# Relative attention stage: another place for four transposes a head, for the relative scores, the row sums and half of the window exponentials, and another order on POOL and on the sync queue

## The chip, the cores and the metric

The kernel runs on one core of a Trainium2 chip. The metric is device time in microseconds (us) for one execution of the whole program; the median of the runs is what is compared. The engines are called PE (TensorE, with its weight loads as PEld), DVE (VectorE), ACT (ScalarE), POOL (GpSimd) and SP (the engine that only issues DMAs here).

## What is computed

A transformer layer: attention with relative positions, then a plain attention and a mixture of experts. The change is in the first part alone. Cut to it (the input x is 2 x 2048 x 256, so there are 2 x 16 = 32 heads of 2048 rows, each 16 wide):

```
B, S, H, NH, MRP = (4, 256, 256, 16, 64)
DK = H // NH
def _rel_idx(seq_len):
    r = jnp.arange(seq_len)
    dist = r[None, :] - r[:, None]
    return jnp.clip(dist, -MRP, MRP) + MRP
nb, seq_len, _ = x.shape
idx = _rel_idx(seq_len)
rk = embK[idx]
rv = embV[idx]
...
logits = jnp.einsum('bhqd,bhkd->bhqk', q, k) + jnp.einsum('bhqd,qkd->bhqk', q, rk)
w = jax.nn.softmax(logits, axis=-1)
out = jnp.einsum('bhqk,bhkd->bhqd', w, v) + jnp.einsum('bhqk,qkd->bhqd', w, rv)
out = out.transpose(0, 2, 1, 3).reshape(nb, seq_len, NH * DK)
return out @ Wo.T + bo
```

Further than 64 columns from the diagonal the relative terms are constants of their side, so they are folded into two versions of k and v. Only a window of 128 columns left and 128 right of each 128-row tile needs the table itself.

## The kernel before

The stage is `rel_attention`. It makes one pass over the 32 heads in a loop of four unrolled heads (p = 0 to 3, eight turns of the loop). One pass through the body for head t is called a period here. In it the engines work on three heads at once: the exponentials and the weighted sum of head t, the maxima of head t+1, and the relative scores of head t+2.

PE sets the beat. A period has 16 steps; each step holds one `weigh` (p times v, L1422), two units of scores for the maxima (L1351, two halves each, into the two buffers psA), and four or five items of RING, which fill the three banks of psS. RING has 68 items a head: 56 blocks of transposed scores for the exponentials ("E", L1391), 8 transposes of the window exponentials ("W", L1397) and 4 transposes of the folded window ("F", c = 0 to 3, L1402). The fills run LEAD = 8 items ahead, so item i stands near step (i - 8) / 4.25. An F fill waits in PE's order for POOL's fold of the same c. Between the units stand four products R (L1361) with the relative table, in the steps of R_STEPS, behind their `weigh`.

DVE takes every psA buffer in PE's order as a turn, 38 a period: 32 maxima (L1225, L1227), the four R copies (`keep_r`, L1244), the gathering of the heads (L1258) and the row of maxima (L1251). After the turns of SUM_TURNS it sums the right half of the window (`sum_right`, L1238), and after turn RC_REL of every second head it inverts the denominators. ACT empties psS (`copy_out`, L1318, an exponential or a copy) and takes the 16 window exponentials of a head between those (`window_exp`, L1322), eight of them ahead, in steps 12 to 15 of the period before, and eight in the period itself.

Two paths lead through DRAM, since they skew rows. For c = 0 to 3:

- scores of head t+2: R copied by DVE, `write_r` (L1010), `read_r` (L1016) once the write has landed and DVE is done with group c of the head before, then `part_r` on POOL (L1137), which masks left and right.
- window of head t: `join_p` on POOL (L1137, L1172) when ACT's exponentials of group c are there, `write_p` (L1020), `read_p` (L1025) when that has landed, `fold_p` on POOL (L1180, L1184), then the F fill on PE.

All these DMAs are issued by SP, in one written order, and so are `load_stack` (nine DMAs of q and k for a head, twice a period), `load_v` (once in four heads), `send_m` (the row of maxima, L1031), and for every second head `gather_denominators` (L1039, L1042), `spread_reciprocals` (L1047, L1050) and `store_o` (L1060). A `wait` in one of them holds whatever is behind it in SP's order. Likewise POOL's order of joins, parts and folds is written out.

## Time and profile before

| | us |
|---|---|
| median of 3 runs | 5036.89 (5022.62 to 5041.27) |
| the profiled execution | 5042.24, its span 5040.5 |
| PE busy, whole span | 4249.3 (84%) |
| DVE busy | 3690.0 (73%) |
| ACT busy | 3016.6 (60%) |
| POOL busy | 1447.1 (29%) |

The relative attention takes the stretch from about 0.25 ms to 2.53 ms; the plain attention and the experts after it are not touched. Shares over the whole span say little, since the stages have different limits. What counts is a single period in the steady part, read engine by engine, with the waits that end last there. Times below are often given as a phase: us since the start of the first `weigh` (step 0) of that period. The head shown most starts at 1236.55 us and is an odd one (p = 1, without the denominators); the next one, even (p = 2), starts at 1301.56 us.

### The profile page before, as it was taken

What the parts mean: (1) busy time and instruction counts of PE and PEld (TensorE: products, weight loads), DVE (VectorE), ACT (ScalarE), POOL (GpSimd) and SP (SyncE); (2) the same over time, 40 slices, a digit from 0 to 9 for tenths busy, and PEclk for the clock granted to TensorE, in tenths of its full rate; (3) what the DMA queues carried; (4) which work ended last, traced back from release to release, by engine and by line L of the source; (5) the groups of instructions that cost most, each with busy time, mean ns of one, the idle gap of its engine ahead of it and who ended that gap; (6) DMA issues with size and microseconds to landing.
All of it is one profiled execution on the core that took longest, in us unless ns stands there. A gap on an engine that the chain in (4) does not pass through costs nothing. (4 is left out here: it accounts for less than half of the span.)

```text
span 5040.5 us, 97058 instructions
## 1 busy us (share of the span) xinstructions
PE 4249.3 (84%) x26882; PEld 2231.3 (44%) x26882; DVE 3690.0 (73%) x6635; ACT 3016.6 (60%) x5838; POOL 1447.1 (29%) x1418
## 2 busy tenths in 40 slices
PE   3778888888888888888846699999999999669997
PEld 1334444444444444444433233333333333459997
DVE  2776777677767676767726788888888888557775
ACT  1226666666666666666601187787787778336664
POOL 0034545554545545545410000000000000142232
PEclk9958889898988888988977699999999999779999
DMA  3755556565656555565554532333223322476664
GB/s 103 229 113 131 129 134 147 132 143 128 139 121 143 137 136 133 135 135 130 132 161 163 113 48 37 44 43 48 39 36 48 49 39 38 103 222 172 171 178 120
DMA packets 512589, 579.74 MB, mean 115 GB/s; under 512 B 71976, under 2 KB 451928, under 8 KB 502000
## 3 DMA queue, kind: packets, MB, share of 16 engines
q1 hardware_dynamic: 453568, 489.90, 43.0%
q10 hardware_dynamic: 38656, 58.73, 3.1%
q0 software_dynamic: 19824, 24.52, 3.0%
q8 instruction: 264, 4.33, 0.4%
q14 instruction: 277, 2.27, 0.2%
HBM read 365.10 MB, written 210.95 MB: 114 GB/s over the span
## 5 line engine op out<-in xcount | busy, mean ns | idle before, releaser
L1225 DVE TENSOR_REDUCE ra_pm<-ra_psA 128x1 f32<-128x896 f32 x1068 | 1162.2, 1088 | 478.5 <-PE ra_psA L1351 462.4
L1318 ACT ACTIVATE ra_p<-ra_psS 128x512 f32<-128x512 f32 x2053 | 1116.2, 604 | 535.0 <-PE ra_psS L1391 275.6
L633 DVE TENSOR_REDUCE pa_pm<-pa_psA 128x2 f32<-128x1024 f32 x1068 | 1261.0, 1219 | 183.6 <-PE pa_psA L724 183.2
L698 ACT ACTIVATE pa_p<-pa_psS 128x512 f32<-128x512 f32 x2054 | 1072.1, 602 | 290.7 <-PE pa_psS L747 263.6
L1351 PE MATMUL ra_psA<-ra_zs,ra_qs 48*128 48x512 f32 x2136 | 918.7, 496 | 111.3 <-DVE ra_rst L1244 58.0
L724 PE MATMUL pa_psA<-pa_zs,pa_qs 48*128 48x512 f32 x2136 | 837.4, 476 | 76.1 <-DVE pa_recb L664 29.9
L747 PE MATMUL pa_psS<-pa_qs,pa_zs 50*128 50x512 f32 x2056 | 823.8, 469 | 51.7 <-ACT pa_p L698 35.2
L1391 PE MATMUL ra_psS<-ra_qs,ra_zs 50*128 50x512 f32 (+3 forms) x2184 | 769.9, 433 | 54.8 <-ACT ra_p L1318 47.6
L1422 PE MATMUL ra_psO<-ra_p,ra_vs 128*32 128x512 f32 (+3 forms) x6400 | 622.1, 497 | 0.0
L747 PEld LDWEIGHTS pa_psS<-pa_qs,pa_zs 50*128 50x128 f32 x2056 | 348.2, 188 | 595.6 <-ACT pa_p L698 562.4
L758 PE MATMUL pa_psO<-pa_p,pa_vs 128*32 128x512 f32 x4096 | 557.6, 617 | 0.0
L1391 PEld LDWEIGHTS ra_psS<-ra_qs,ra_zs 50*128 50x128 f32 x2184 | 363.7, 195 | 363.8 <-ACT ra_p L1318 296.6
L1351 PEld LDWEIGHTS ra_psA<-ra_zs,ra_qs 48*128 48x128 f32 x2136 | 378.6, 202 | 320.2 <-DVE ra_pm L1227 122.8
L724 PEld LDWEIGHTS pa_psA<-pa_zs,pa_qs 48*128 48x128 f32 x2136 | 366.7, 192 | 247.8 <-DVE pa_pm L633 148.7
L612 POOL COPY pa_vs<-pa_vall 128x256 f32 (+1 forms) x33 | 13.2, 399 | 1310.6 <-PE pa_psO L758 1074.6
L2224 PE MATMUL mo_psH<-mo_hp,mo_w_parts 128*128 128x384 f32 x1392 | 284.5, 340 | 5.9 <-DVE mo_w_parts L2310 5.9
L2238 PE MATMUL mo_psY<-mo_w_parts,mo_hid_parts 128*128 128x256 f32 x2088 | 283.7, 281 | 0.0
L2238 PEld LDWEIGHTS mo_psY<-mo_w_parts,mo_hid_parts 128*128 128x128 f32 x2088 | 272.3, 189 | 3.8 <-DVE mo_hid_parts L2380 0.2
L1180 POOL TENSOR_TENSOR ra_blk<-ra_blk 128x508 f32<-128x508 f32 x128 | 161.8, 1264 | 381.1 <-DMA ra_blk<-window_rows 376.1
L1422 PEld LDWEIGHTS ra_psO<-ra_p,ra_vs 128*32 128x32 f32 x6400 | 203.9, 114 | 147.8 <-ACT ra_p L1318 54.6
L2195 POOL DMA_INDIRECT acc_rows<-mo_y,mo_ids x87 | 154.2, 1772 | 384.4 <-DVE mo_y L2365 366.7
L1137 POOL TENSOR_TENSOR ra_pc<-ra_sw,masks 128x512 f32<-128x512 f32 (+2 forms) x160 | 169.4, 1059 | 277.8 <-DVE ra_sr L1238 248.5
(250 smaller groups left out, 5306.6 us busy)
## 6 DMA issues: line engine op xcount, KB each, us to landing
relative_rows<-ra_rst SPq DMA_DIRECT2D x136, 512.0 KB, 4.0
ra_blk<-window_rows SPq DMA_DIRECT2D x128, 512.0 KB, 4.6
mo_w_raw<-ffn_W SPq DMA_DIRECT2D x58, 1024.0 KB, 5.5
ra_dl<-relative_rows SPq DMA_DIRECT2D x136, 256.0 KB, 3.2
window_rows<-ra_pc SPq DMA_DIRECT2D x128, 256.0 KB, 4.3
pa_qs<-q_halves SPq DMA_DIRECT2D x210, 128.0 KB, 5.5
pa_zs<-kl_halves SPq DMA_DIRECT2D x210, 128.0 KB, 5.9
ra_qs<-q_halves SPq DMA_DIRECT2D x204, 128.0 KB, 3.8
```

What stands on the lines that cost most here:

```text
L633: dve.reduce_max(pm[:, par, 2 * a:2 * a + 2], psA[w][:, :, :], AX.X).then_inc(s_am.h, 1)
L698: act.activation(pr[:, i % NPR, :], psS[:, slot(i), :], ACT.Exp).then_inc(s_ex.h, 1)
L724: last = pe.matmul(psA[w][:, half, :], qs[0:PR, k % U, i * P:(i + 1) * P], zs[0:PR, k % U, e * G:(e + 1) * G], start=True, stop=True)
L747: pe.matmul(psS[:, slot(i), :], zs[at:at + PR + NP2, p % U, z * P:(z + 1) * P], qs[at:at + PR + NP2, p % U, c * G:(c + 1) * G], start=True ...
L758: last = pe.matmul(psO[32 * m:32 * m + 32, :], vs[:, p % 2, 4 * (k % 4) + m, :], pr[:, (4 * k + m) % NPR, :], start=k % 4 == 0, stop=k % 4 ...
L1225: dve.reduce_max(pm[:, q, i, 2 * left:2 * left + 1], psA[w][:, lo:lo + 2 * G - P], AX.X).then_inc(s_far.h, 1)
L1318: act.activation(dst, psS[:, slot(i), :], ACT.Exp if kind == "E" else ACT.Copy).then_inc(s_cp.h, 1)
L1351: last = pe.matmul(psA[w][:, half * G:(half + 1) * G], qs[0:PR, q, i * P:(i + 1) * P], zs[0:PR, q, at:at + G], start=True, stop=True)
L1391: last = pe.matmul(dst[:, lo:hi], zs[at:at + PR + NP2, q, z * P:(z + 1) * P], qs[at:at + PR + NP2, q, c * G + lo:c * G + hi], start=True, ...
L1422: last = pe.matmul(psO[32 * m:32 * m + 32, lo:hi], v[:, z, :], pr[:, (4 * k + m) % NPR, lo:hi], start=n == 0, stop=n == 3, tile_position=( ...
L2224: last = pe.matmul(psH[:, u % 3, 0:BT], w1[:, q, x, c, f * P:(f + 1) * P], hp[:, q, z, c, :], start=c == 0 and m == 0, stop=c == CH - 1 an ...
L2238: last = pe.matmul(psY[:, j, 0:D], hid[:, x, u % NHID, j * P:(j + 1) * P], w2[:, q, z, f, :], start=f == 0 and m == 0, stop=f == FC - 1 an ...
```

## The change

No instruction is added or removed. Six things are moved:

- The four F fills go from ring places 32, 41, 50, 59 to 38, 43, 52, 63.
- R goes from steps 0, 1, 4, 5 to steps 0, 3, 6, 8.
- The second eight window exponentials go from two a step in steps 0 to 3 to one a step in steps 0 to 7; the eight ahead stay.
- The four sums go from turns 8, 10, 12, 14 to 5, 9, 14, 25, the inversion from turn 20 to 17.
- SP's order is another one, and so is POOL's.

```
-for _c, _at in reversed(tuple(enumerate((32, 40, 48, 56)))):
+for _c, _at in reversed(tuple(enumerate((38, 42, 50, 60)))):
     RING.insert(_at, ("F", _c, 0))
-R_STEPS = (0, 1, 4, 5)
+R_STEPS = (0, 3, 6, 8)
-WX_STEP, WX_PER = 12, 2
+WX_STEPS = (12, 12, 13, 13, 14, 14, 15, 15) + tuple(range(STEPS, STEPS + 8))
-RC_REL = 20
-SUM_TURNS = (8, 10, 12, 14)
+RC_REL = 17
+SUM_TURNS = (5, 9, 14, 25)
...
-        k, ahead = WX_STEP + j // WX_PER, 1
+        k, ahead = WX_STEPS[j], 1
...
                     read_r(t + 2, p, 0)
-                    write_r(t + 2, p, 1)
+                    if p % 2 == 0:
+                        gather_denominators(t, n)
                     write_p(t, p, 1)
                     read_p(t, p, 0)
-                    write_p(t, p, 2)
+                    write_r(t + 2, p, 1)
                     read_p(t, p, 1)
                     read_r(t + 2, p, 1)
-                    write_p(t, p, 3)
+                    write_p(t, p, 2)
                     if p % 2 == 0:
-                        gather_denominators(t, n)
+                        spread_reciprocals(n)
                     write_r(t + 2, p, 2)
-                    write_r(t + 2, p, 3)
                     if p == 2:
                         load_v(t + 2, 4 * (t + 2))
+                    read_p(t, p, 2)
                     read_r(t + 2, p, 2)
-                    read_p(t, p, 2)
-                    if p % 2 == 0:
-                        spread_reciprocals(n)
-                    read_p(t, p, 3)
+                    write_r(t + 2, p, 3)
+                    write_p(t, p, 3)
                     read_r(t + 2, p, 3)
                     load_stack(t + 3, p + 1, 0, s_qa)
+                    read_p(t, p, 3)
                     send_m(t + 1, p + 1)
...
-                    for c in range(4):
-                        join_p(t, p, c)
-                    for c in range(2):
-                        part_r(t + 2, c)
-                    for c in range(4):
-                        fold_p(t, c)
-                    for c in range(2, 4):
-                        part_r(t + 2, c)
+                    join_p(t, p, 0)
+                    join_p(t, p, 1)
+                    part_r(t + 2, 0)
+                    join_p(t, p, 2)
+                    fold_p(t, 0)
+                    fold_p(t, 1)
+                    part_r(t + 2, 1)
+                    part_r(t + 2, 2)
+                    join_p(t, p, 3)
+                    fold_p(t, 2)
+                    fold_p(t, 3)
+                    part_r(t + 2, 3)
```

What that makes of SP's queue in the later part of an even head (p = 0). The semaphores s_rw2 and s_pw3 tell that `write_r` 2 and `write_p` 3 have landed, s_rec that the denominators are inverted. Before:

```order
L1010 DMA relative_rows<-ra_rst 128x4x256 [waits ra_s_rc]
...
L1016 DMA ra_dl<-relative_rows 128x4x128 [waits ra_s_am,ra_s_rw2]
...
L1025 DMA ra_blk<-window_rows 128x4x256 [waits ra_s_fl,ra_s_pw2]
...
L1047 DMA reciprocals<-ra_rec 128x32 [waits ra_s_rec]
...
L1025 DMA ra_blk<-window_rows 128x4x256 [waits ra_s_fl,ra_s_pw3]
...
L1016 DMA ra_dl<-relative_rows 128x4x128 [waits ra_s_am,ra_s_rw3]
...
L995 DMA ra_zs<-kl_halves 16x1984 x3
...
L1031 DMA ra_qs<-ra_mrow 1x16x128 [waits ra_s_mr]
```

and in the changed kernel:

```order
L1047 DMA reciprocals<-ra_rec 128x32 [waits ra_s_rec]
...
L1010 DMA relative_rows<-ra_rst 128x4x256 [waits ra_s_rc]
...
L1025 DMA ra_blk<-window_rows 128x4x256 [waits ra_s_fl,ra_s_pw2]
...
L1016 DMA ra_dl<-relative_rows 128x4x128 [waits ra_s_am,ra_s_rw2]
...
L1020 DMA window_rows<-ra_pc 128x4x128 [waits ra_s_pc]
...
L1016 DMA ra_dl<-relative_rows 128x4x128 [waits ra_s_am,ra_s_rw3]
...
L995 DMA ra_zs<-kl_halves 16x1984 x3
...
L1025 DMA ra_blk<-window_rows 128x4x256 [waits ra_s_fl,ra_s_pw3]
...
L1031 DMA ra_qs<-ra_mrow 1x16x128 [waits ra_s_mr]
```

The reciprocals now stand ahead of `write_r` 2, and the last `read_p` now stands behind the nine DMAs of `load_stack`.

POOL, the last join of a head (the one with 128x384 in it) and what stands ahead of it. Before:

```order
L1172 TENSOR_TENSOR ra_pc<-ra_pc,ra_tmp 128x512 [waits ra_s_ps]
...
L1137 TENSOR_TENSOR ra_pc<-ra_sw,masks 128x512 [waits ra_s_sr,ra_s_pw1,ra_s_we]
...
L1137 TENSOR_TENSOR ra_tmp<-ra_sw,masks 128x384 [waits ra_s_ps]
...
L1137 TENSOR_TENSOR ra_dr<-ra_dl,masks 128x512 [waits ra_s_rr0]
```

and in the changed kernel:

```order
L1137 TENSOR_TENSOR ra_dr<-ra_dl,masks 128x512
L1137 TENSOR_TENSOR ra_dl<-ra_dl,masks 128x512
...
L1137 TENSOR_TENSOR ra_pc<-ra_sw,masks 128x512
...
L1137 TENSOR_TENSOR ra_tmp<-ra_sw,masks 128x384
...
L1172 TENSOR_TENSOR ra_pc<-ra_pc,ra_tmp 128x512
...
L1180 TENSOR_TENSOR ra_blk<-ra_blk 128x4x127
L1184 TENSOR_TENSOR ra_blk<-ra_blk,ra_sr 128x4
```

The last join now stands behind `part_r` 2 (the first two rows), and the folds 2 and 3 stand right behind that join.

## Rows read from the trace of the kernel before

**Rows 1.** Busy time in stretches (us, busy, instructions; PEclk is the granted clock).

```profile
core 0: us, PE busy (x) PEld busy (x) DVE busy (x) ACT busy (x) POOL busy (x), PEclk, DMA share, GB/s
1236.50:1301.50 65.00, 57.66 (x415) 28.65 (x413) 49.00 (x108) 44.39 (x90) 33.91 (x37) 0.89 0.59 135
1256.20:1269.80 13.60, 10.15 (x40) 4.45 (x38) 6.47 (x13) 3.21 (x6) 10.34 (x12) 0.50 0.64 190
```

**Rows 2.** Who waited for whom, whole span (us in total, times, longest).

```profile
POOL ra_pc L1137 <- DVE ra_sr L1238: 248.5, 32, 15.6
...
PE ra_psS L1402 <- POOL ra_blk L1184: 136.5, 32, 6.3
```

**Rows 3.** The tile ra_nm, written once a head.

```profile
L1234 DVE TENSOR_REDUCE ra_nm<-ra_pm x33: 219/220/222, 316.1 to 2493.1; 128x16 f32<-128x64 f32 x33
```

**Rows 4.** Timeline of PE, head at 1236.55: start, length, operation, idle before.

```profile
1236.55 1.07 PE L1422 MATMUL ra_psO<-ra_p,ra_vs 128*32 128x512 f32 x8
...
1252.16 1.07 PE L1422 MATMUL ra_psO<-ra_p,ra_vs 128*32 128x512 f32 x8
...
1257.31 1.94 PE L1422 MATMUL ra_psO<-ra_p,ra_vs 128*32 128x512 f32 x8
...
1266.03 1.09 PE L1402 MATMUL ra_psS<-ident,ra_blk 128*128 128x128 f32 x4 [3.44 <-POOL ra_blk L1184]
...
1291.21 1.06 PE L1422 MATMUL ra_psO<-ra_p,ra_vs 128*32 128x512 f32 x8
...
1301.56 1.07 PE L1422 MATMUL ra_psO<-ra_p,ra_vs 128*32 128x512 f32 x8
```

**Rows 5.** Timeline of POOL, the same head: last join, parts 0 and 1, first fold.

```profile
1254.29 1.28 POOL L1137 TENSOR_TENSOR ra_pc<-ra_sw,masks 128x512 f32<-128x512 f32 x1 [0.24 <-POOL ra_pc L1172]
...
1258.72 1.27 POOL L1137 TENSOR_TENSOR ra_dr<-ra_dl,masks 128x512 f32<-128x512 f32 x1 [0.18 <-POOL ra_pc L1172]
...
1261.67 1.27 POOL L1137 TENSOR_TENSOR ra_dr<-ra_dl,masks 128x512 f32<-128x512 f32 x1
...
1264.35 1.25 POOL L1180 TENSOR_TENSOR ra_blk<-ra_blk 128x508 f32<-128x508 f32 x1
```

**Rows 6.** Timeline of SP, the same head: first write and read, last read, stack, maxima.

```profile
1239.57 0.40 SPq L1010 DMA_DIRECT2D relative_rows<-ra_rst  x1
...
1245.89 0.36 SPq L1016 DMA_DIRECT2D ra_dl<-relative_rows  x1
...
1281.20 0.36 SPq L1016 DMA_DIRECT2D ra_dl<-relative_rows  x1
1281.99 1.33 SPq L995 DMA_DIRECT2D ra_qs<-q_halves  x3
...
1286.55 1.20 SPq L1031 DMA_DIRECT2D ra_qs<-ra_mrow  x2
```

**Rows 7.** Timeline of SP, the even head at 1301.56: v loads and reciprocals.

```profile
1329.29 0.79 SPq L1003 DMA_DIRECT2D ra_vg<-v_rows  x1
...
1334.15 0.45 SPq L1016 DMA_DIRECT2D ra_dl<-relative_rows  x1
...
1339.89 0.34 SPq L1047 DMA_DIRECT2D reciprocals<-ra_rec  x1
...
1344.42 0.39 SPq L1025 DMA_DIRECT2D ra_blk<-window_rows  x1
```

**Rows 8.** DMA issues: operation, count, KB each, median us to landing.

```profile
relative_rows<-ra_rst SPq DMA_DIRECT2D x136, 512.0 KB, 4.0
ra_blk<-window_rows SPq DMA_DIRECT2D x128, 512.0 KB, 4.6
...
ra_dl<-relative_rows SPq DMA_DIRECT2D x136, 256.0 KB, 3.2
...
ra_qs<-ra_mrow SPq DMA_DIRECT2D x66, 8.0 KB, 5.9
pa_qs<-pa_mrow SPq DMA_DIRECT2D x66, 8.0 KB, 1.8
```

**Rows 9.** Timeline of DVE, the same odd head: a copy of R between turns.

```profile
1254.04 1.22 DVE L1244 COPY ra_rst<-ra_psA 128x1024 f32<-128x1024 f32 x1
```

**Rows 10.** Timeline of PE at the edge of the loop body (fourth head to first).

```profile
1162.59 0.50 PE L1351 MATMUL ra_psA<-ra_zs,ra_qs 48*128 48x512 f32 x1 [2.95 <-issue]
```

## The prediction

> **What bounds the kernel now.** The change touches one stage, so I left the shares of the whole span aside and read in this order: how long a head takes, which engine is full within a head, where that engine waits, and which chain ends last at that wait. The row of maxima is made once a head, 33 times from 316.1 to 2493.1 us [rows 3]: 32 periods of 68.0 us, 2177 us in all. An undisturbed odd head goes from the weigh at 1236.55 to that at 1301.56, 65.0 us [rows 4]. In it PE is busy for 57.66 us, DVE 49.00, ACT 44.39, POOL 33.91 [rows 1]. So PE is the bound, and nobody else is near 65. What PE loses lies in one place. At phase 29.5 (1266.03) the transpose F of c = 0 comes after 3.44 us of idle time, released by POOL's fold [rows 4]; over all heads that wait is 136.5 us in 32 times, 4.3 us a head [rows 2]. Around it the granted clock is 0.50, that is 1.2 instead of 2.4 GHz, from 1256.2 to 1269.8, with 10.15 us of PE work in it [rows 1]. Once in four heads the loop's edge costs 2.95 us more and a slow stretch [rows 10].
>
> The chain behind the wait: POOL makes the fold at 1264.35, behind four joins and two parts [rows 5], and the joins themselves were late, since join 2 waits for DVE's sum 0 (248.5 us in 32 times, 7.8 us a head [rows 2]). This idle time of POOL ends in the wait of PE.
>
> **What PE would take without waits.** Step 4 begins at phase 15.6 (1252.16). The last three steps, from 1291.21 to 1301.56, run at full clock with two transposes W in them and take 10.35 us [rows 4], 3.45 us a step. Fifteen point six and twelve such steps are 57 us. That is 8 us a head, 256 us in all, to be had if nothing else is late.
>
> **Part by part.** *The edits with one answer.* The eight exponentials move from steps 0 to 3 to steps 0 to 7. ACT has 20 us of idle time in a head [rows 1] and the work is the same; W of c = 2 stands in step 9 and wants its four by step 3. I cost it at nothing; if ACT's cover is gone, it is one exponential, half a microsecond, and no more. The sums 0 and 1 come earlier and cost DVE the same; join 2 can then start some 5 us earlier, and fold 0 stands behind three joins and one part instead of four and two. F0 itself moves 6 ring items later. So the wait of 4.3 us goes; I take that as certain, for fold 0 is then ready near phase 21 (odd heads) or 22 (even), and F0 is wanted near 25.
>
> *R two to three steps later.* The third R was DVE's turn 12, at 1254.04, phase 17.5, ahead of any slow stretch [rows 9]: 1.46 us a turn. It is turn 16 now, so it starts near 23.3 and is copied by 24.6. The least would be 16 turns of 1.22 us, the length of that copy, ready by 20.7; the most is that a slow stretch stays, 28. I take 24.6, by the nearest row.
>
> *What now stands in a row behind it.* `write_r` 2 at 24.8, landed 4.0 later; `read_r` 2, landed 3.2 later [rows 8]; `part_r` 2 on POOL, 2.7 us like part 1 (1261.67 to 1264.35); then join 3, which the change has put behind that part, 4.4 us (1254.29 to 1258.72) [rows 5]. Join 3 is done at J = 39.1. Fold 2 needs 1.5 us more, so F2 is free at 40.7, while it is wanted in step 10, behind its weigh, near 37.5. A wait of some 3 us.
>
> In even heads the reciprocals stand ahead of `write_r` 2. The inversion is behind turn 17, so done near 26.2. The spreading holds SP from 1339.89 to 1344.42, 4.5 us [rows 7], until 30.7. Then J = 30.9 + 4.0 + 3.2 + 2.7 + 4.4 = 45.2. In one head of four `load_v` stands there too, 1329.29 to 1334.15, 4.9 us [rows 7]; `read_r` 2 is then issued at 36.7 instead of 34.9, and J = 47.0. In before the same wait for the reciprocals held only the last `read_p`, and nobody waited for that.
>
> *The last read behind the stack.* This weighs most. With join 3 done at J, SP issues `write_p` 3, `read_r` 3, then nine DMAs of the stack (1281.99 to 1286.4), then `read_p` 3: from `read_r` 3 to there is 5.3 us (1281.20 to 1286.55) [rows 6], so J + 5.8. How long it takes to land the trace does not show in this place. Alone it takes 4.6 us. The row of maxima, 8 KB, issued behind the same stack, takes 5.9, and 1.8 in the other attention, where no such stack is ahead of it: 4.1 us of queueing [rows 8], and 4.6 + 4.1 = 8.7. The first `write_r`, 512 KB behind the other stack, was waited for from 1239.57 to 1245.89, 6.3 us [rows 6], though issued a microsecond further behind. I take 7.5, between the two, with 4.6 and 9.5 as ends. Then fold 3, 1.5 us: F3 is free at J + 14.8. PE wants it in step 13, two and a half steps after F2, at J + 1.6 + 8. A second wait of 5 us. Who is queued behind it on PE: everything of three more steps.
>
> *From F3 to the end of the head.* As in before from 1291.21 to 1301.56, 10.35 us, and 1.0 for F3 and the rest of its step: 11.4. The wait brings a slow clock. In before it stayed at 0.50 from the restart at 1266.03 to 1269.8 [rows 1, 4], 3.8 us that count half: 1.9. I take 2.0.
>
> **The sum.** A head takes J + 14.8 + 11.4 + 2.0 = J + 28.2: 67.3 for each of two odd heads, 73.4 and 75.2 for the even ones, against 65.0 in before, the loop's edge being left as it is. That is 2.3 + 2.3 + 8.4 + 10.2 = 23.2 us in four heads, eight times: 186 us. On the profiled execution's 5042 us this gives 5228, and against the median, 5 us lower, 5223.
>
> So the gain of 4.3 us at F0 is real, and is given back at F2 and F3.
>
> **Rivals.** (1) *The clock stays low for longer.* If two waits in a head hold it at 0.50 for as much work as in before, 10.15 us of it, 5.1 us are lost instead of 2.0: 3.1 x 32 = 99 us more, 5322. For it: in before the clock fell ahead of the wait, in a stretch full of R and W. Against: R is now spread over steps 0 to 8. The Trainium skill's page "TensorE: Matmul & The Clock Gate", section Terms, prices a throttled stretch at its length times (1 - K/N), half here. On the 13.6 us stretch that would be 6.8 us, and the time 5223 + 4.8 x 32 = 5377; the trace has PE idle for 3.4 us of that stretch, so I stay with 5.1.
>
> (2) *The reads are quick enough.* If `read_p` 3 lands in 4.6 us, as alone (2.9 less), and there is no slow stretch (2.0 less), 0.9 of the mean 5.8 us a head is left; R a microsecond sooner takes it away. The time is then 5037, no change. For it: the DMA queues are only 0.59 busy [rows 1]. Against: the 5.9 us of the 8 KB row.
>
> (3) *PE runs free: faster.* Were fold 3 done by phase 46 and fold 2 by 37.5, a head would take 57 us and the kernel 5037 - 256 = 4781. It decides at `read_p` 3: it must be issued by phase 38 or so, when in SP's order even join 3 is not done. Half of that gain, 4910, would need the chain from R to join 3 shorter by 6 us. Turns at 1.22 us would give 4.
>
> (4) *The F0 wait stays.* It would only add; fold 0 has 3 us to spare, so I give it nothing of its own.
>
> **How the numbers follow.** The forecast has 58 in 100, the longer slow stretch 18, no change 10, faster 14 (all the way 6, part of it 8). 0.5% (25 us) is about what a measurement of this kernel tells from no change. So slower by over that: 0.76; within it: 0.10; faster: 0.14. Ends of the unknown terms: the landing -2.9 or +2 us a head (-93, +64), the slow stretch -2 or +3.1 (-64, +99), R up to -4. The range goes from 5020 to 5340; it leaves out the faster cases and the far end of the first rival.
>
> **What would show it.** In the profile after: the wait of PE's F fill on POOL's fold should be no less than in before, 250 us or so in 60 times, and stand at c = 2 and 3; POOL should wait for the last `read_p` for about 10 us a head; POOL's wait for DVE's sum should be gone; SP's last `read_p` should stand behind the stack with 7 us or more to landing; heads should be 67 and 73 to 75 us long in turn. The prediction is wrong if F3 finds its fold done, or if even heads are no longer than odd ones.

## The result: slower by 6.6%, 1.8 times the loss forecast

| | before | after |
|---|---|---|
| median, us | 5037.3 (5022.62 to 5041.27, 4 runs) | 5369.16 (5340.55 to 5382.8, 4 runs) |
| ratio to before | | 1.0657, 95% interval 1.0609 to 1.0705 |
| relative attention, first to last row of maxima, us | 2177.0 | 2457.2 |
| the same for each of 32 heads | 68.0 | 76.8 |

The forecast was 5223 (5020 to 5340): slower, as it came out, but by 186 us where 332 were lost. All rows below are of the profiled executions, 5042.24 us before and 5340.55 after: the second is the quickest of its four, so there are 298 us between them, and not 332. The page of the profile after, its first lines and the granted clock in 40 slices:

```profile
span 5338.8 us, 97058 instructions
...
PE 4370.9 (82%) x26882; PEld 2307.9 (43%) x26882; DVE 3692.3 (69%) x6635; ACT 3046.6 (57%) x5838; POOL 1446.8 (27%) x1418
...
PEclk9868888787878887887867769999999999869999
```

PE's share of the span fell, and yet PE is busy 122 us longer, with no instruction added. The stage alone, by after's row of maxima (before's is [rows 3]):

```profile
L1238 DVE TENSOR_REDUCE ra_nm<-ra_pm x33: 219/220/222, 318.3 to 2775.5; 128x16 f32<-128x64 f32 x33
```

The window between its ends, with the columns of [rows 1], in before:

```profile
316.10:2493.10 2177.00, 1891.82 (x13120) 937.37 (x13120) 1576.40 (x3477) 1415.16 (x2797) 1130.37 (x1175) 0.87 0.59 136
```

and in after:

```profile
318.30:2775.50 2457.20, 2000.58 (x13124) 1010.73 (x13128) 1576.99 (x3475) 1444.64 (x2798) 1129.66 (x1173) 0.81 0.54 120
```

The stage is 280 us longer. PE is busy for 109 us of that, and the granted clock went from 0.87 to 0.81. The rest is waiting. Who waited for whom (us in total, times, longest), after, whole span:

```profile
POOL ra_blk L1180 <- DMA ra_blk<-window_rows: 524.2, 65, 17.3
...
PE ra_psS L1406 <- POOL ra_blk L1184: 260.9, 56, 9.5
```

In after's stage alone, PE for POOL (the folds) and for DVE (the copies of R, the maxima):

```profile
PE ra_psS L1406 <- POOL ra_blk L1184: 253.9, 55, 9.5
PE ra_psA L1355 <- DVE ra_rst L1248: 82.4, 130, 3.2
PE ra_psA L1355 <- DVE ra_pm L1231: 55.7, 83, 1.7
```

and the last two in before, in its stage (its waits for the folds all lie in the stage):

```profile
PE ra_psA L1351 <- DVE ra_rst L1244: 43.2, 66, 3.2
...
PE ra_psA L1351 <- DVE ra_pm L1227: 20.5, 69, 0.5
```

PE's wait for the folds was 136.5 us in 32 times [rows 2] and is 260.9 in 56, 253.9 of it in the stage: 117 more there. Of after's waits, 108 us stand in step 10 (fold 2) and 153 in step 12 (fold 3). PE's waits for DVE, which copies R and takes the maxima, went from 64 to 138 us: 74 more. 109 + 117 + 74 = 300, against 280; PE's waits for ACT got 12 us shorter (47 to 35), and I did not follow the last 8. POOL's wait for DVE's sum [rows 2] is gone; it waits for the reads of the window instead, 524 us (376 in before).

Windows of after, an odd head from 1341.2 (the first five) and the late part of the even one from 1413.9:

```profile
1341.20:1363.20 22.00, 19.90 (x159) 10.15 (x157) 18.34 (x39) 16.15 (x32) 15.73 (x15) 1.00 0.88 193
1363.20:1369.60 6.40, 4.99 (x31) 2.49 (x29) 5.06 (x11) 4.09 (x8) 4.18 (x5) 0.82 0.29 97
1369.60:1380.00 10.40, 9.94 (x56) 5.16 (x55) 5.36 (x11) 4.44 (x8) 4.60 (x4) 0.50 0.25 77
1380.00:1395.00 15.00, 14.07 (x97) 7.19 (x97) 11.32 (x29) 10.38 (x22) 3.40 (x5) 0.85 0.69 139
1395.00:1401.40 6.40, 0.07 (x2) 0.04 (x1) 1.12 (x3) 0.80 (x2) 1.47 (x3) 0.74 0.56 109
...
1453.50:1462.70 9.20, 0.09 (x5) 0.05 (x1) 1.64 (x4) 0.04 (x1) 7.94 (x8) 0.64 0.23 74
1462.70:1476.90 14.20, 11.68 (x59) 6.00 (x60) 6.96 (x17) 8.04 (x16) 1.52 (x3) 0.50 0.82 139
1476.90:1492.20 15.30, 14.56 (x81) 6.96 (x81) 7.70 (x18) 9.65 (x20) 6.86 (x8) 0.68 0.24 43
```

The odd head has two faults. In the second row a step of 6.4 us holds only 5 us of PE's work, and the clock falls in it (at 1367.3), ahead of any wait for a fold; the third row is at 0.50 (1.2 GHz) with PE busy for 9.94 of 10.4 us. And in the fifth row PE does nothing for 6.3 us. The even head waits for 9 us from 1453.5, and then runs at 0.50 and 0.68 until it ends. PE's timeline at these places (columns of [rows 4]):

```profile
1365.98 0.49 PE L1355 MATMUL ra_psA<-ra_zs,ra_qs 48*128 48x512 f32 x1 [1.00 <-DVE ra_pm L1231]
...
1401.37 1.12 PE L1406 MATMUL ra_psS<-ident,ra_blk 128*128 128x128 f32 x4 [6.33 <-POOL ra_blk L1184]
...
1462.68 1.09 PE L1406 MATMUL ra_psS<-ident,ra_blk 128*128 128x128 f32 x4 [9.12 <-POOL ra_blk L1184]
```

What lies behind F3 in the odd head, on POOL:

```profile
1380.82 1.27 POOL L1172 TENSOR_TENSOR ra_pc<-ra_pc,ra_tmp 128x512 f32<-128x512 f32 x1
...
1399.78 1.25 POOL L1180 TENSOR_TENSOR ra_blk<-ra_blk 128x508 f32<-128x508 f32 x1 [16.06 <-DMA ra_blk<-window_rows]
```

and on SP:

```profile
1379.78 0.36 SPq L1010 DMA_DIRECT2D relative_rows<-ra_rst  x1
1382.12 0.38 SPq L1020 DMA_DIRECT2D window_rows<-ra_pc  x1
1386.31 0.36 SPq L1016 DMA_DIRECT2D ra_dl<-relative_rows  x1
1387.42 1.34 SPq L995 DMA_DIRECT2D ra_qs<-q_halves  x3
...
1391.85 0.41 SPq L1025 DMA_DIRECT2D ra_blk<-window_rows  x1
```

and on DVE, the last of the 32 maxima of head t+1:

```profile
1384.92 1.09 DVE L1229 TENSOR_REDUCE ra_pm<-ra_psA 128x1 f32<-128x896 f32 x1 [2.44 <-PE ra_psA L1355]
1385.93 0.28 DVE L1231 CUSTOM_DVE_ANT_0 ra_sw<-ra_psA,ra_dl 128x128 f32<-128x128 f32 x1
```

The last join is done at J = 1382.09. `write_r` 3 has landed by 1382.67, but `read_r` 3 also waits for DVE to be done with the group that it overwrites: the last maximum is done at 1386.2, the read goes out at 1386.31. The stack stands behind it, and `read_p` 3 is issued at 1391.85, J + 9.8 (the median of such heads is J + 7), and has landed by 1399.78. So the chain is the one forecast, with more in it.

**A measure of the clock for what follows.** Each trace has a record of granted clock. I counted in the stage how long it stood at 0.50: 575 us in before, 18.0 a head, and 950 us in after, 29.7 a head. (The windows give about the same: 2 x (1 - 0.87) x 68.0 = 17.7 and 2 x (1 - 0.81) x 76.8 = 29.2.) PE was busy for 448 and 783 us of that; half of it, 7.0 and 12.2 us a head, is my estimate of what the clock cost, since a `weigh` of eight matmuls takes 1.07 us at 1.00 and 1.93 at 0.50.

### The profile page after: what moved, and what is told of

The parts are those of the page before. It is cut to its first block and busy times, and to the rows that moved or that the text cites. A ratio compares the mean times of both kernels' runs of the same rounds, so it can differ in the third digit from the quotient of the medians.

```text
span 5338.8 us, 97058 instructions
## 1 busy us (share of the span) xinstructions
PE 4370.9 (82%) x26882; PEld 2307.9 (43%) x26882; DVE 3692.3 (69%) x6635; ACT 3046.6 (57%) x5838; POOL 1446.8 (27%) x1418
## 5 line engine op out<-in xcount | busy, mean ns | idle before, releaser
L1355 PE MATMUL ra_psA<-ra_zs,ra_qs 48*128 48x512 f32 x2136 | 948.4, 524 | 182.4 <-DVE ra_rst L1248 98.4
L1395 PE MATMUL ra_psS<-ra_qs,ra_zs 50*128 50x512 f32 (+3 forms) x2184 | 833.6, 469 | 38.7 <-ACT ra_p L1322 35.5
L1426 PE MATMUL ra_psO<-ra_p,ra_vs 128*32 128x512 f32 (+3 forms) x6400 | 676.1, 536 | 0.0
L1355 PEld LDWEIGHTS ra_psA<-ra_zs,ra_qs 48*128 48x128 f32 x2136 | 414.1, 220 | 395.5 <-DVE ra_rst L1248 158.8
L1395 PEld LDWEIGHTS ra_psS<-ra_qs,ra_zs 50*128 50x128 f32 x2184 | 408.8, 217 | 338.7 <-ACT ra_p L1322 185.7
L1406 PE MATMUL ra_psS<-ident,ra_blk 128*128 128x128 f32 x512 | 118.3, 373 | 261.3 <-POOL ra_blk L1184 260.9
L1137 POOL TENSOR_TENSOR ra_dr<-ra_dl,masks 128x512 f32<-128x512 f32 (+2 forms) x170 | 179.4, 1055 | 517.2 <-DMA ra_dl<-relative_rows 510.3
L1426 PEld LDWEIGHTS ra_psO<-ra_p,ra_vs 128*32 128x32 f32 x6400 | 221.2, 121 | 157.7 <-ACT ra_p L1322 64.9
```

Source lines behind the costliest of these rows:

```text
L1355: last = pe.matmul(psA[w][:, half * G:(half + 1) * G], qs[0:PR, q, i * P:(i + 1) * P], zs[0:PR, q, at:at + G], start=True, stop=True)
L1395: last = pe.matmul(dst[:, lo:hi], zs[at:at + PR + NP2, q, z * P:(z + 1) * P], qs[at:at + PR + NP2, q, c * G + lo:c * G + hi], start=True, ...
L1426: last = pe.matmul(psO[32 * m:32 * m + 32, lo:hi], v[:, z, :], pr[:, (4 * k + m) % NPR, lo:hi], start=n == 0, stop=n == 3, tile_position=( ...
```

## The experiments

"Slow" is the time at 0.50 a head, "F waits" PE's wait for the folds over the whole span. Each ratio is to the kernel before, run beside it (its medians there were 5033 to 5048). The interval of c1 is wide because its four runs go from 4893.86 to 4975.79.

| run | median us | ratio (95%) | stage | slow | F waits |
|---|---|---|---|---|---|
| before | 5037.3 | | 2177.0 | 18.0 | 136.5 |
| after | 5369.16 | 1.0657 | 2457.2 | 29.7 | 260.9 |
| a1 | 5146.14 | 1.0212 (1.0170 to 1.0255) | 2282.4 | 22.7 | 130.4 |
| a2 | 5276.28 | 1.0457 (1.0416 to 1.0499) | 2421.1 | 31.6 | 190.8 |
| a3 | 5246.63 | 1.0402 (1.0360 to 1.0444) | 2372.3 | 28.3 | 171.6 |
| a4 | 5004.85 | 0.9944 (0.9917 to 0.9970) | 2126.5 | 17.8 | 9.2 |
| a5 | 4932.82 | 0.9804 (0.9777 to 0.9831) | 2041.1 | 11.4 | 22.7 |
| a6 | 5074.74 | 1.0078 (1.0051 to 1.0105) | 2209.1 | 23.5 | 8.3 |
| b1 | 5055.96 | 1.0027 (0.9991 to 1.0062) | 2175.8 | 22.6 | 38.6 |
| b2 | 4887.29 | 0.9695 (0.9667 to 0.9723) | 2013.6 | 11.1 | 21.1 |
| c1 | 4906.64 | 0.9769 (0.9691 to 0.9848) | 2018.0 | 12.3 | 3.0 |
| c2 | 4898.31 | 0.9705 (0.9663 to 0.9747) | 2035.0 | 11.5 | 32.0 |
| c3 | 5294.96 | 1.0514 (1.0459 to 1.0569) | 2417.5 | 28.0 | 237.8 |
| c4 | 5359.88 | 1.0568 (1.0487 to 1.0649) | 2461.3 | 27.6 | 72.3 |
| d1 | 5354.04 | 1.0603 (1.0569 to 1.0637) | 2471.1 | 32.6 | 261.1 |
| d2 | 4885.03 | 0.9689 (0.9663 to 0.9715) | 2024.4 | 11.9 | 25.0 |
| d3 | 5391.61 | 1.0692 (1.0647 to 1.0738) | 2506.0 | 34.9 | 244.8 |

### From after backwards: the three places in the queues

**a1**, the last read ahead of the stack on SP:

```
                     read_r(t + 2, p, 3)
-                    load_stack(t + 3, p + 1, 0, s_qa)
                     read_p(t, p, 3)
+                    load_stack(t + 3, p + 1, 0, s_qa)
```

> The changed kernel with one edit: the last read of the window rows is issued ahead of the nine DMAs of the stack, as before the change, and nothing else. In the changed kernel that read was issued 7.2 us after the last join and took 8.2 to 9 us to land. Theory 1 (the second wait of PE in a head, at the fold of c = 3, is made by this read's place behind the stack): issued at some 4.2 us after the join, since it then waits for the landing of the write, and landed 5 us later, the fold is ready 6 us sooner; the wait of PE there nearly goes, with part of the slow clock: 5369 falls by 5 to 8 us a head, to 5110 to 5210. Theory 2 (the low clock of 24 to 31 us a head comes from the new spread of relative products and transposes over the steps, whatever is waited for): 5340 or more, the slow stretches as long as they are.

Measured: 223 us of the 332 are back. `read_p` 3 is issued at phase 43.3 to 43.5 in odd heads and 50.4 to 51.8 in even ones, and lands 4.7 us later; in after it was issued at 48 and at 52.8 to 54.2, and took 8.0 to 9.0. PE's wait for the folds is halved (waits, as above):

```profile
PE ra_psS L1406 <- POOL ra_blk L1184: 130.4, 32, 10.3
```

130 us of wait went, and 223 us of time; the slow stretches went from 29.7 to 22.7 us a head with it. What went is the wait in step 12, for fold 3: 153 us before, 4 now; that in step 10, for fold 2, is 127 us (108). The last read behind the stack is the largest single part of the loss.

**a2**, the reciprocals back behind `read_r` 2:

```
-                    if p % 2 == 0:
-                        spread_reciprocals(n)
                     write_r(t + 2, p, 2)
...
                     read_r(t + 2, p, 2)
+                    if p % 2 == 0:
+                        spread_reciprocals(n)
```

> The changed kernel with one edit: the spreading of the reciprocals goes behind the third read of the relative rows, and nothing else. Theory 1 (even heads are longer because it stands ahead of the third write of the relative rows and holds the sync queue until 31 us): the last join of an even head comes 6 us sooner, and the even heads are as long as the odd ones: 16 heads by 6 us, about 100 us, 5270. Theory 2 (even heads are longer by something else, the clock or the loads of v): over 5340, the last join of even heads where it was, at 46 to 48 us.

Measured: 93 us back. The last join of even heads is now done at 41.7 to 43.7 instead of 47 to 48. The slow time did not fall (31.6).

**a3**, the last join ahead of `part_r` 2 on POOL:

```
                     part_r(t + 2, 1)
-                    part_r(t + 2, 2)
                     join_p(t, p, 3)
+                    part_r(t + 2, 2)
```

> The changed kernel with one edit: on POOL the last join stands ahead of the third part of the relative rows, and nothing else. Theory 1 (the join is late because of that part, which waits for a read of what DVE copies in step 6): the last join is done near 30 us instead of 41 to 48, the wait of PE at c = 2 is gone (3.4 us in odd, 9 us in even heads), while the last read still stands behind the third and fourth relative reads and the stack, so it lands near 53 and PE still waits at c = 3: 5369 less some 6 us a head, 5180. Theory 2 (POOL's order matters little, since the join also waits for the exponentials that come one a step): the last join at 36 or later and 5330 or more.

Measured: 123 us back. The last join now starts its add at 29 to 34.6, but F3 still waits, for its read stands behind `read_r` 3 and the stack: an early join is worth only part of the loss while SP's order holds the read. (The three singles add up to 439 us, more than the 364 of the three together: they share some of the waiting.)

**a4**, all three:

> The changed kernel with the three edits of the other runs together: the last window read ahead of the stack, the reciprocals behind the third relative read, the last join ahead of the third part. Ring places, steps of the relative products, exponentials, sums and the rest of both orders are as changed. Theory 1 (the ring and the turns are sound, only the queues behind them are not): both waits of PE go, the slow clock shrinks to the loop's edge, and a head takes 57 to 60 us: 4780 to 4900, under the kernel before. Theory 2 (the clock falls because of the spread of relative products and transposes): the waits go but 15 us or more of slow clock a head stay, and the time is 5050 or more.

Measured: 364 us back and the kernel 0.6% faster than before; the wait for the folds in its trace:

```profile
PE ra_psS L1406 <- POOL ra_blk L1184: 9.2, 8, 2.5
```

and the window of its stage:

```profile
318.80:2445.30 2126.50, 1900.73 (x13117) 952.83 (x13119) 1572.08 (x3476) 1442.42 (x2797) 1131.30 (x1173) 0.87 0.60 139
```

So three places in two written orders make the whole loss. The time lies between the two that were written down for it, 4780 to 4900 and 5050 or more. Left in a4 are the later R, the F places, the sums and the exponentials, and a clock no better than before's, though PE hardly waits for a fold any more.

**a5**, a4 with the third sum three turns later, out of the turns of the third R:

```
-SUM_TURNS = (5, 9, 14, 25)
+SUM_TURNS = (5, 9, 17, 25)
```

> The combined version (last window read ahead of the stack, reciprocals behind the third relative read, last join ahead of the third part), with one more edit: DVE's sum 2 behind turn 17 instead of turn 14, out of the way of the relative product of step 6, which in every head has a wait of 1.0 us at phase 24.8 and makes step 6 last 5.4 us. Theory 1 (queues alone): the combined version less 0.6 us a head, 4985. Theory 2 (a crowded step makes the clock fall: 17 us of slow clock from phase 26 on in some heads): these stretches from phase 26 on go as well, 4900 to 4960.

Measured: 72 us more, 2.0% faster than before; PE's wait for the maxima in the stage fell by a third and the clock rose to 0.91, in the window of its stage:

```profile
316.60:2357.70 2041.10, 1820.21 (x13124) 925.91 (x13128) 1568.92 (x3475) 1437.20 (x2798) 1133.55 (x1173) 0.91 0.62 145
```

**a6**, a4 with the exponentials back at two a step:

```
-WX_STEPS = (12, 12, 13, 13, 14, 14, 15, 15) + tuple(range(STEPS, STEPS + 8))
+WX_STEPS = (12, 12, 13, 13, 14, 14, 15, 15) + (16, 16, 17, 17, 18, 18, 19, 19)
```

> The combined version with the second eight window exponentials back at two a step in steps 0 to 3. If the spreading of the exponentials is worth nothing by itself, as predicted: 5005 within 25. If it relieves ACT where ACT is full: steps 0 to 3 longer, 5030 or more. If it keeps the last join and ACT's steps 4 to 7 late: 4980 or less.

Measured: 70 us slower than a4. So in a4's setting the spread of the exponentials is worth 70 us; it was costed at nothing. The likely way, not tested by itself, is that two of them a step push back ACT's emptying of psS: step 0 of every fourth head (p = 3) took 5.3 us instead of 3.8, eight slow stretches begin in step 0 where a4 has none, and the slow time grew to 23.5 us a head.

### From before forwards: one part alone

**b1**, the kernel before with the F places of after:

```
-for _c, _at in reversed(tuple(enumerate((32, 40, 48, 56)))):
+for _c, _at in reversed(tuple(enumerate((38, 42, 50, 60)))):
```

> The kernel before with one edit: the four F transposes at the ring places of the changed kernel (38, 43, 52, 63 for 32, 41, 50, 59). F0 is wanted some 6 items, 5 us, later, and POOL's fold is where it was, at phase 29. Theory 1 (PE's wait at F0 is worth its own length and the slow clock behind it): the wait shrinks from 4.3 us a head to about 1 or none, the slow clock of 10 to 14 us with it, 5037 falls to 4850 to 4930. Theory 2 (the slow stretch starts at phase 19.5, ahead of the wait, and is made by the dense steps of R and W; the wait only fills it): 4980 to 5010, the slow clock stays at 10 us or more a head.

Measured: no change, 1.0027 (0.9991 to 1.0062), above both expectations. The wait is mostly gone:

```profile
PE ra_psS L1402 <- POOL ra_blk L1184: 38.6, 13, 3.0
```

and the stage is as long as it was:

```profile
316.60:2492.40 2175.80, 1981.87 (x13125) 999.23 (x13129) 1578.52 (x3477) 1424.82 (x2798) 1130.85 (x1174) 0.83 0.59 136
```

98 us of wait became 90 us more of PE's busy time, with the same instructions: the clock fell from 0.87 to 0.83. What is left of the wait is 13 waits of about 3 us, all in step 6. One of them, in PE's timeline:

```profile
1170.68 1.08 PE L1402 MATMUL ra_psS<-ident,ra_blk 128*128 128x128 f32 x4 [2.96 <-POOL ra_blk L1184]
```

and the windows ahead of it, of it and behind it:

```profile
1163.00:1167.00 4.00, 3.76 (x27) 1.77 (x25) 4.00 (x7) 2.34 (x5) 3.59 (x5) 1.00 0.42 124
1167.70:1170.70 3.00, 0.04 (x2) 0.05 (x1) 0.77 (x3) 0.81 (x2) 2.77 (x4) 0.94 0.56 184
1170.70:1184.00 13.30, 13.30 (x68) 6.67 (x68) 6.66 (x16) 5.98 (x11) 2.85 (x4) 0.50 0.53 159
```

The clock falls at the end of the wait and stays at 0.50 for 13.3 us in which PE is never idle. It does so at all 13: it falls within the last 0.9 us of the wait and comes back 9.3 to 13.5 us behind it (once 3.4).

**b2**, the kernel before with folds 0 and 1 ahead of parts 0 and 1 on POOL:

```
                         join_p(t, p, c)
                     for c in range(2):
+                        fold_p(t, c)
+                    for c in range(2):
                         part_r(t + 2, c)
-                    for c in range(4):
+                    for c in range(2, 4):
                         fold_p(t, c)
```

> The kernel before with one edit: on POOL the folds 0 and 1 stand ahead of the parts 0 and 1 (still behind the four joins). Fold 0 is then done near phase 24 instead of 29, F0 is wanted near 25. Theory 1: the same gain as by moving F0, 4850 to 4930. Theory 2 (dense steps make the slow stretch): 4980 to 5010. If the parts, now 3 us later, held DVE at the groups 0 and 1 of the head after next, it would be slower; they are wanted from step 10 on, phase 45, and done by 27, so neither theory expects it.

Measured: 3.0% faster than before, faster than every kernel here but d2, its twin. In the head from 1155.9, on POOL:

```profile
1177.99 1.27 POOL L1180 TENSOR_TENSOR ra_blk<-ra_blk 128x508 f32<-128x508 f32 x1
```

on PE:

```profile
1179.69 0.63 PE L1404 MATMUL ra_psS<-ident,ra_blk 128*128 128x128 f32 x4 [0.47 <-POOL ra_blk L1184]
```

and the window around it:

```profile
1177.90:1185.00 7.10, 6.61 (x61) 3.66 (x60) 6.31 (x13) 4.53 (x9) 6.37 (x9) 1.00 0.89 274
```

The fold starts at phase 22.1 instead of 27.8 [rows 5], F0 waits for 0.47 us instead of 3.44 [rows 4], and the clock stays at 1.00 throughout this head. 115 us of wait went, and 150 us of time. The crowded step is as it was: 19 of the 33 slow stretches of b2 begin in step 4, against 27 of 51 in before.

**c1**, b2 with the F places of after (the edit of b1):

> The kernel before with the folds 0 and 1 ahead of the parts 0 and 1 (4887 us by itself) and also the ring places of the changed kernel (no gain by themselves, 5056, though PE's wait fell from 136.5 to 38.6 us). Theory 1 (the ring places only matter through the wait at F0; that is gone already): 4887 within 25. Theory 2 (the transposes crowd the other steps at the new places and make the clock fall): 4930 or more, with a longer slow clock than the 12 us a head of the fold run.

**c2**, b2 with `R_STEPS = (0, 1, 3, 6)`:

> The kernel before with the folds 0 and 1 first, and the relative products in steps 0, 1, 3, 6 instead of 0, 1, 4, 5, so that none of them shares a step with a transpose of the window after step 1. Theory 2 (the clock falls after a crowded step: in the fold run it falls at phase 19.5, after step 4 with a product and a transpose): the slow stretches from phase 19 on go, 4800 to 4850. Theory 1 (only waits matter; there is none at phase 19): 4880 to 4900.

Measured: c1 0.9769 (0.9691 to 0.9848), c2 0.9705 (0.9663 to 0.9747), against 0.9695 of b2. Neither adds anything. But c1 and b1 have the same F places and differ in POOL's order alone, and c1 is 149 us faster. In its stage:

```profile
PE ra_psS L1404 <- POOL ra_blk L1184: 3.0, 2, 1.6
```

```profile
317.30:2335.30 2018.00, 1845.31 (x13124) 936.35 (x13128) 1578.34 (x3476) 1418.33 (x2798) 1133.26 (x1174) 0.90 0.64 147
```

The clock is 0.90 against b1's 0.83, PE is busy 137 us less, and no slow stretch begins in step 6, where b1 has 13. So the F places do not lower the clock by themselves: what b1 lost there came with the late fold and the 3 us waits that it left.

**c3**, b2 with `R_STEPS = (0, 3, 6, 8)`, those of the change:

> The kernel before with the folds 0 and 1 first, and the relative products at the changed kernel's steps 0, 3, 6, 8; the queues' order is of before. The fourth write of the relative rows waits until phase 33 and stands ahead of two reads of the window rows in the sync queue. Theory 1 (later products alone make the late chain, whatever the queue's order): fold 2 at 41 or later, wanted at 38: a wait of 3 us or more a head, 4950 to 5050. Theory 2 (the products spread over free steps make it shorter, the wait stays under 1 us): 4880 or less.

Measured: 408 us slower than b2, nearly as slow as after, with SP's order of before; both times written down for it (4950 to 5050, 4880) are missed. PE's waits, of which 108 us stand in step 5 (F0) and 130 in step 9 (F2):

```profile
PE ra_psS L1404 <- POOL ra_blk L1184: 237.8, 64, 7.6
```

A later R, then, does the same harm without the change's orders: the written queue of before holds `read_p` 0 behind `write_r` 1 and `read_p` 2 behind `write_r` 3. In heads p = 1, `write_r` 3 is now issued at 42.9 and `read_p` 2 at 44.0, against 26.6 in b2; POOL's wait for the reads of the window is 548 us, against 219. In a4 the same R steps stand beside an order with `read_p` 2 ahead of `write_r` 3, and it is issued at 27.2. The later R and the orders have to be judged together.

### What lowers the clock

**c4**, after, with eight useless matmuls ahead of F2 and sixteen ahead of F3, into the bank that F overwrites. They are added work, of no use to the result:

```
+                    for _ in range((0, 0, 8, 16)[c]):
+                        pe.matmul(dst, zs[64:64 + PR + NP2, q, 0:P], qs[64:64 + PR + NP2, q, 0:G], start=True, stop=True)
```

> The changed kernel with 8 more matmuls ahead of the transpose F2 and 16 ahead of F3 of every head, of 512 columns and 0.22 us each at full clock (1.8 and 3.5 us), into the bank that the transposes then overwrite, ahead of the wait for the fold: PE does useless work where it stood idle. Nothing else is changed, and the folds are ready when they are. Theory 1 (the idle time itself makes the slow clock of 26 us a head, of which the busy part is lost by half): the slow clock shrinks by 10 us or more a head and the time falls by 2 to 5 us a head, to 5200 to 5300. Theory 2 (the slow clock comes from crowded steps): the added work costs what does not fit in the waits, 5369 to 5450, slow clock as before.

Measured: 5359.88, against 5369.16 of after. One wait of PE with its filling, in PE's timeline (columns of [rows 4]):

```profile
1395.17 3.90 PE L1405 MATMUL ra_psS<-ra_qs,ra_zs 50*128 50x512 f32 x16
...
1400.90 0.66 PE L1408 MATMUL ra_psS<-ident,ra_blk 128*128 128x128 f32 x4 [1.84 <-POOL ra_blk L1184]
```

the waits of the whole span:

```profile
PE ra_psS L1408 <- POOL ra_blk L1184: 72.3, 29, 7.9
```

and the stage:

```profile
317.70:2779.00 2461.30, 2189.38 (x13869) 1150.97 (x13873) 1576.82 (x3476) 1444.49 (x2798) 1130.95 (x1173) 0.82 0.53 120
```

PE is busy for 189 us more, the idle waits are down from 261 to 72 us, the stage is as long as it was (2461.3 and 2457.2), and the clock is 0.82 instead of 0.81. So filling most of the wait did not bring the clock back. The test is not clean: 29 waits of up to 7.9 us are left, and the filling is only one kind of work. But here eight of the 19 slow stretches that begin in step 12 do so with PE at work throughout the 3 us ahead, on the filling for the most part: idle time is not the only thing that goes with a fall.

**d1**, after with the third sum at turn 17 (the edit of a5):

> The changed kernel with one edit: DVE's sum 2 behind turn 17 instead of 14, so that step 6 has the relative product, F0 and no sum. If a crowded step makes the clock fall (it falls at phase 26 in half of the heads, right behind step 6, with no wait of PE on a fold there): the stretches from phase 26 on get rarer, slow clock 25 us a head or less instead of 29.7, time 5270 to 5320. If the waits for folds 2 and 3 decide alone, nothing changes but 0.6 us a head: 5350.

**d3**, after with F0 at place 40 instead of 38:

> The changed kernel with one edit: F0 at ring place 40 instead of 38, so that it comes after the weigh of step 7 and not in the same interval as the relative product and the sum. Crowded step: the interval from step 6 to 7 falls from 5.4 to 4.7 us, the stretches from phase 26 on get rarer, 5270 to 5320. Waits alone: 5350 to 5390.

Measured: d1 5354.04 and d3 5391.61, slow time 32.6 and 34.9 a head. Both thin out the step in which the clock first falls, and neither helps in after: the forecasts of the crowded step (5270 to 5320) are missed.

**d2**, b2 with `SUM_TURNS = (8, 10, 14, 17)`:

> The kernel before with the folds 0 and 1 first (4887) and DVE's sums 2 and 3 behind turns 14 and 17 instead of 12 and 14; turn 12 is the relative product of step 4, and the clock falls at phase 19.5, behind that step. Crowded step: the stretches from 19.5 on go in part, slow clock 8 us a head or less instead of 11.1, 4820 to 4870. If only waits counted: 4887 within 15, or more if fold 2, which needs sum 2, came late.

Measured: 4885.03, the same as b2 (0.9689 and 0.9695).

Counting where the slow stretches begin, in before most begin in step 4 (27), then 5 (14) and 15 (10); in after in step 12 (25), 10 (17) and 6 (16). Steps 10 and 12 are where F2 and F3 wait; step 6 is the one with the third R, the third sum and F0. Two things go with a fall, then. One is a wait of PE for a fold: b1 shows it 13 times out of 13, and taking out the last waits took slow time with them (b1 22.6, c1 12.3; after 29.7, a1 22.7, a4 17.8), though from before to b1, which leaves 3 us waits, it rose (18.0 to 22.6). The other is a crowded step: in before all 27 falls of step 4 come ahead of the wait, with no idle time of PE over 0.4 us just before. Thinning such a step out paid once (a5, 72 us); in c2, d1, d3 and d2 it missed the times written down for it. What exactly the chip reacts to stays open.

## Why the forecast was right in its sign and short in its size

**The queue chain: right, each link somewhat short.** Medians over 20 heads, those of one p taken together:

| step of the prediction | forecast | measured |
|---|---|---|
| third R copied | 24.6 | 25.9, and 28.9 in p = 0 |
| J, odd heads | 39.1 | 40.9 |
| J, p = 0 and 2 | 45.2 and 47.0 | 48.1 and 47.0 |
| last `read_p` issued | J + 5.8 | J + 5.8 to 7.1 |
| its landing | 7.5 (4.6 to 9.5) | 8.0 to 9.0 |
| fold 3 done | J + 14.8 | J + 16 to 17.4 |
| PE's wait for folds, whole span | 250 us or so in 60 times | 260.9 in 56 |
| POOL's wait for the last `read_p` | 10 us | 13 to 14, 16.06 in the head shown |
| length of a head, p = 0, 1, 2, 3 | 73.4, 67.3, 75.2, 67.3 | 80.3, 72.8, 78.5, 78.4 |

The link left out is `read_r` 3 ahead of the stack. In most heads it is issued 0.6 us behind `write_p` 3, as forecast; in five of the ten odd ones it waits for DVE's last maximum, up to 4.9 us behind `write_p` 3 (4.2 in the head shown), with the stack and `read_p` 3 behind it. DVE takes that maximum from PE's scores, which come late where PE's steps are slow: in heads p = 1 steps 6 to 8, at half clock, take 5 to 6 us each, against 3.8 to 5.4 in p = 3. The slow clock lengthens the very chain that makes PE wait. The landing was taken between two rows; the further of the two, 8.7, was right. The row on PE's wait looks like a hit and is none: the next paragraph has why.

**The clock: the term that failed.** "The wait brings a slow clock ... I take 2.0": this prices the slow clock at 2.0 us a head, as something that follows one wait and lasts 3.8 us. Measured, it costs 12.2 us a head in after and 7.0 in before. The starting point, 57 us a head without waits, held well: a head less PE's F wait in the stage and less the half of its busy time at 0.50 is 56.8 us in before, 56.6 in after, and 55.6 to 57.8 in all the other runs but c4, which has added work (61.8). With that, the sum can be taken apart. By its own terms (F2 wanted at 37.5, free at J + 1.6, and 5.2 us of wait at F3) it holds 8.4 us of waiting in each odd head and 14.5 and 16.3 in the even ones, 11.9 on average and 381 us in all, and not the "250 us or so" that stands beside it. Measured are 7.9 a head in the stage. And it is taken against the 65.0 us of the head in [rows 1, 4], in which the half of 10.15 us at 0.50 is 5.1.

| us a head | forecast, change to before | measured, change to before |
|---|---|---|
| waits for folds | 3.4 to 11.9: +8.5 | 4.3 to 7.9: +3.7 |
| slow clock | 5.1 to 2.0: -3.1 | 7.0 to 12.2: +5.2 |
| whole head | +5.8 | +8.8 |

So the forecast let the clock's cost fall by 3.1 us, since it has no term for slow work ahead of the waits, where it rose by 5.2, and had the waits grow too much. The two belong together: the sum has PE at step 10 at full speed, at 37.5, in every head. In after it begins at 38.5 in p = 2 and 3, and at 47.7 and 42.3 in p = 0 and 1, where slow steps stand ahead of it, and part of the forecast wait is spent in them. (57 against the 56.5 of that head makes up the rest of the 5.8.) That the total came within 3.0 us a head is in part luck: the errors have opposite signs. The first rival (5322, and 5377 by the Trainium skill's page "TensorE: Matmul & The Clock Gate", section Terms) had the mechanism, and its times were the nearer; but its price too was put on one stretch a head, where there are two, after step 6 and after steps 10 to 12. As to the page's price, the length of the throttled stretch times one half would be 14.8 us a head here; PE is idle for part of it, and the busy part gives 12.2.

**F0's wait goes: right, and worth less than its length.** It is gone in after (no wait for a fold ahead of step 10); in b1 alone 98 of its 136.5 us go. But "8 us a head to be had if nothing else is late" was not had by moving F0 alone: b1 gave it all back in clock. b2, which moves POOL's fold instead, got 150 us.

**The exponentials cost nothing: wrong, in the other direction.** With the queues mended they gain 70 us (a6 against a4); in the change as it stands they were not tested. Late exponentials alone in the kernel before were not tried: there they would hold the last join on POOL, with F0 behind it.

**R a microsecond later: too small.** The third copy itself was late by 1.3 us (4.3 in p = 0), as a number right enough. But PE's waits around the R copies and maxima doubled, 64 to 138 us, which the forecast did not have; they stay in a4, where the queues are mended (85 and 64 us). Against the later R as such speaks c3.

**The other rivals.** Quick reads (5037) fell: 8.0 to 9.0 us. A free PE (4781) would have needed `read_p` 3 by phase 38; after issues it at 48 in odd heads and later in even ones. Its price fell too: in a4 and c1 PE waits for the folds for 9.2 and 3.0 us in all, and they take 5005 and 4907, since 8.5 and 5.8 us a head of slow clock stay. That even heads are longer than odd ones holds against p = 1; p = 3 is as long as p = 2, and the loop's edge lies in it.

## What to carry to other kernels

A written queue order and the step that feeds it are one edit: moving a producer later (R) cost 408 us where the window's reads stand behind its writes (c3 against b2), and was borne where `read_p` 2 stands ahead of the last of them (a4), so list for each moved step what is queued behind its waits. Where the granted clock falls inside the period, a wait's price is not its length: removing 98 us of idle gained nothing (b1) and removing 115 gained 150 (b2), so forecast the busy time at half clock as a term of its own, with the one of before as the start, and never take a head that has it against a sum that has not. Try the reordering that brings the late producer forward before the one that moves its consumer back.

## What was new about the hardware

- The clock can take back a removed wait in full. b1: waits 136.5 to 38.6 us, PE busy 1891.8 to 1981.9 us, stage 2177.0 to 2175.8. Taking the last 36 us of wait out as well (c1: 3.0 us left) gave 158 us of the stage.
- A wait of 3 us can be followed by far more than 3 us of half clock, 9.3 to 13.5 us behind 12 of the 13 waits of b1, and PE is busy for all 13.3 us in the head shown.
- Keeping PE busy in most of the waits did not keep the clock up. c4: waits 261 to 72 us, PE busy 189 us more, slow time 29.7 to 27.6 us a head, and the time did not change.
- A DMA issued behind the nine of the stack landed late, in both sizes seen: 8 KB take 5.9 us in before (1.8 in the other attention, [rows 8]), 512 KB 8.0 to 9.0 in after (4.7 ahead of them in a1). That is 3.3 to 4.3 us more. The DMA engines are busy for only 0.54 of the stage, but for 0.83 to 0.88 of the time in which that read is on its way; in a1 it is 0.75 to 0.82, so that share alone doesn't tell the landing. In after the 8 KB stand behind the 512 KB too, and take 6.9 us (columns of [rows 8]):

```profile
ra_qs<-ra_mrow SPq DMA_DIRECT2D x66, 8.0 KB, 6.9
```
